# The last layer of a graph network: Strassen's seven products in place of eight, per pair of row tiles

## The reference

```python
h = relu(layernorm(x));  x = x + L0(h, adj)     # (A @ (h W0 + b0)) / column sums
h = relu(layernorm(x));  x = x + L1(h, adj)     # normalised A + I, relu
h = relu(layernorm(x));  x = x + L2(h, adj)     # attention over adj
h = relu(layernorm(x));  x = x + L3(h, adj)
# L3: head = mask / sqrt(row sum of mask); inc = adj + head
#     return (inc @ h) / sum(inc)               # = adj @ h times one factor per row
```

## Time and profile before

| | |
|---|---|
| median of 3 runs | 1386.33 us (1385.8 to 1390.24) |
| profiled execution, own time | 1388.27 us |
| its span | 1386.4 us |
| busy: PE, weight loads, DVE, ACT, POOL | 1344.6, 1023.1, 861.2, 528.8, 118.5 us |

### The profile page before, as it was taken

How to read it: one execution, slowest core, us unless ns; L and a number is a source line. 1 busy time by engine, 2 the same in 40 slices (tenths; PEclk the granted TensorE clock), 3 DMA queues, 4 the chain that set the end, 5 groups by cost and what they waited for, 6 DMA issues and landing times.

```text
span 1386.4 us, 26434 instructions
## 1 busy us (share of the span) xinstructions
PE 1344.6 (97%) x10252; PEld 1023.1 (74%) x10252; DVE 861.2 (62%) x1776; ACT 528.8 (38%) x1240; POOL 118.5 (9%) x193
## 2 busy tenths in 40 slices
PE   4899999989999999999999999999999999999999
PEld 3688888864555555567777777777777777888887
DVE  5799888958355555577677767767777886000000
ACT  3487544726222222344444544544545553000000
POOL 1100000012323222210000000000000000000000
PEclk8899999999999999999999999999999999999999
DMA  9999999720121120101110111110111003232221
GB/s 225 254 314 348 378 378 379 288 81 16 61 61 52 56 62 1 62 24 32 31 31 24 31 39 32 31 31 24 32 39 32 16 24 122 85 92 85 84 85 31
DMA packets 52812, 141.19 MB, mean 102 GB/s; under 512 B 7632, under 2 KB 16848, under 8 KB 52688
## 3 DMA queue, kind: packets, MB, share of 16 engines
q1 hardware_dynamic: 50288, 137.39, 31.2%
q10 hardware_dynamic: 2400, 2.10, 0.4%
HBM read 118.49 MB, written 20.97 MB: 101 GB/s over the span
## 4 chain that ended last, share of the span: by engine, by line
PE 88%; DVE 6%; DMA 2%; SPq 1%; issue 1%; ACT 1%; POOL 0%; DVEq 0%; ACTq 0%
PE ps L1336 16%; PE ps L1337 16%; PE ps L1350 11%; PE ps L1237 8%; PE ps L1238 8%; PE ps L1199 7%; PE ps L1200 7%; PE ps L1367 4%; PE ps L1386 4%; PE ps L1398 4%; DMA acc<-in_adj 2%; DVE ring L625 1%; SPq L307 1%; PE ps L1216 1%; PE ps L1295 1%
## 5 line engine op out<-in xcount | busy, mean ns | idle before, releaser
L1199 PE MATMUL ps<-val_hi,ring 128*128 128x257 f16 x1024 | 226.6, 274 | 0.0
L1200 PE MATMUL ps<-val_lo,ring 128*128 128x256 f16 x1024 | 226.5, 273 | 0.0
L1337 PE MATMUL ps<-acc,ring 128*128 128x256 f16 x1024 | 225.8, 273 | 0.0
L1336 PE MATMUL ps<-acc,ring 128*128 128x256 f16 x1024 | 225.8, 271 | 0.0
L1237 PE MATMUL ps<-ring,acc 128*128 128x512 fp8e4 x512 | 194.9, 381 | 4.0 <-DVE acc L762 3.9
L1350 PE MATMUL ps<-hnt 128*128 128x512 f16 (+3 forms) x864 | 196.3, 363 | 0.0
L1238 PE MATMUL ps<-ring,acc 128*128 128x512 fp8e4 x512 | 194.8, 380 | 0.0
L625 DVE STREAM_TRANSPOSE ring<-acc 128x1024 uint8<-128x1024 uint8 x128 | 151.5, 1219 | 27.1 <-DMA acc<-in_adj 26.9
L1142 ACT ACTIVATE ring<-ring 128x512 f16<-128x512 f32 (+2 forms) x133 | 79.3, 596 | 227.1 <-DVE ring L897 226.8
L897 DVE SCALAR_TENSOR_TENSOR ring<-ring,ps 128x512 f32<-128x512 fp8e4 (+2 forms) x133 | 85.7, 645 | 117.5 <-PE ps L1386 117.5
L1336 PE MATMUL ps<-val_hi,hs 128*128 128x257 f16 x534 | 145.8, 273 | 0.6 <-DVE hs L878 0.6
(11 more groups left out here) (166 smaller groups left out, 2104.4 us busy)
## 6 DMA issues: line engine op xcount, KB each, us to landing
acc<-in_adj SPq DMA_DIRECT2D x256, 256.0 KB, 7.7
ring<-at_dram SPq DMA_DIRECT2D x56, 512.0 KB, 3.9
at_dram<-ring SPq DMA_DIRECT2D x32, 512.0 KB, 8.9
ring<-at_dram SPq DMA_DIRECT2D x64, 256.0 KB, 2.9
xs<-in_x SPq DMA_DIRECT2D x12, 256.0 KB, 11.9
out<-xs ACTq DMA_DIRECT2D x14, 128.0 KB, 3.9
out<-xs SPq DMA_DIRECT2D x14, 128.0 KB, 3.1
xs<-in_x SPq DMA_DIRECT2D x8, 128.0 KB, 2.9
```

What stands on the lines that cost most here:

```text
L1199: nc.tensor.matmul(ps[:, k % 8, 0:D + 1], lhs, val_hi0[:, t, 0:D + 1], start=(t == 0), stop=False)
L1200: last = nc.tensor.matmul(ps[:, k % 8, 0:D], lhs, val_lo0[:, t, :], start=False, stop=(t == NB - 1))
L1336: nc.tensor.matmul(ps[:, bank, 0:n], lhs, hi[:, t, 0:n], start=start, stop=False)
L1337: return nc.tensor.matmul(ps[:, bank, 0:D], lhs, lo[:, t, :], start=False, stop=stop)
```

## The change

Row tiles are taken in 16 pairs `n`, one tile of group 2p and the one at the same place in group 2p + 1. The blocks of even and of odd value tiles make with the two row tiles a 2 x 2 matrix, the even and odd value tiles with their left and right 128 columns another. Strassen's scheme multiplies these with seven products instead of eight. A product is 16 matmuls of 256 moving columns (128 high, 128 low).

- Four of the seven stationary operands are differences of adjacency blocks (`d5`, `d1`, `d2`, and `a21`, `a12` changed in place): the 8-bit numbers are so coded that masks and exclusive or on 32-bit words give the differences. For pairs of groups p = 0 part of this stands in attention steps (`PREP`), the rest after the tails; for p > 0 it stands between the products.
- The moving operands are the values and five sums of them, made in f32 with the rows (`make_sums`) and split in high and low (`sums_high`, `sums_low`). The tail has 17 items instead of 15.
- The results are put together by ACT (four copies out of PSUM), GpSimd (two differences) and DVE.
- The adjacency is loaded in 16 pieces of 1 MB, each in runs of 512 bytes.
- Semaphores of the statistics are merged, which changes no order.

```diff
-        TAIL = 15
+        TAIL = 17
-            per = 1 if length > TAIL else 2 if length > GB else 3
+            per = 1 if length >= TAIL else 2 if 2 * length >= TAIL else 3
+        PREP = {}
+        for r in range(4):
+            PREP[16 + 4 * r] = ("mask", "a11", r)
+            PREP[17 + 4 * r] = ("sign", "a11", r)
+            PREP[18 + 4 * r] = ("mask", "a22", r)
+            PREP[19 + 4 * r] = ("sign", "a22", r)
+            PREP[NB + 17 + r] = ("d5", "d5", r)
+            PREP[NB + 21 + r] = ("d7", "a12", r)
...
+            sp.wait_ge(sem["pv1_done"], NS)
+            for k in ("11", "22", "12"):
+                load_raw(sp, 1, k)
...
+                if n % GB == GB - 1 and n // GB + 2 < NG // 2:
+                    sp.wait_ge(sem["products_done"], 4 * n + 4)
+                    load_raw(sp, n // GB + 2, "11")
+                    load_raw(sp, n // GB + 2, "22")
...
+            def make_sums(k):
+                nc.vector.tensor_tensor(sums32[k % 2][:, P:3 * P], even, odd, ALU.add)
+                nc.vector.scalar_tensor_tensor(sums32[k % 2][:, 3 * P:5 * P].rearrange("p (s d) -> p s d", s=2), both[:, :, 0:P], -1.0,
+                                               both[:, :, P:D], ALU.mult, ALU.subtract)
+                nc.vector.tensor_tensor(sums32[k % 2][:, 0:P], even[:, 0:P], odd[:, P:D], ALU.subtract).then_inc(sem["sums_made"], 1)
...
+            def dif2(p):
+                if p > 0:
+                    dve.wait_ge(sem["three_done"], GB * p)
...
+            def first_differences(n):
+                dve.wait_ge(sem["products_done"], 4 * n + 2)
+                dve.wait_ge(sem["copied"], 4 * n + 4)
...
+            dif2(0)
+            dif1(0)
+            dif6(0)
...
+            for n in range(NB // 2):
+                p, i = n // GB, n % GB
+                last = p == NG // 2 - 1
+                if p > 0 and i == 0:
+                    dif7(p)
+                    if not last:
+                        edge_mask(p + 1, "a11")
+                elif i == 1 and p > 0 and not last:
+                    edge_mask(p + 1, "a22")
+                    sign(p + 1, "a11")
+                    sign(p + 1, "a22")
+                elif i == 2 and p > 0 and not last:
+                    dif5(p + 1)
+                    dif1(p + 1)
+                elif i == 3 and not last:
+                    if p == 0:
+                        dif5(1)
+                        dif1(1)
+                    dif2(p + 1)
+                    if p > 0:
+                        dif6(p + 1)
+                first_differences(n)
+                if n == 0:
+                    edge_mask(1, "a11")
+                elif n == 1:
+                    edge_mask(1, "a22")
...
+                two_tiles(n)
...
+            def last_four(n):
...
+                since(pe, sem["tiles_step"], 8 * (n - 1) + 7)
+                pe.wait_ge(sem["difs_done"], 3 * p + 2)
...
+                pe.wait_ge(sem["tiles_step"], 8 * n + 2)
+                pe.wait_ge(sem["dif7_done"], made(p))
...
+                for k in range(12):
+                    pe.wait_ge(sem["lo3_done"], k + 1)
+                    for m in range(3):
+                        multiply(n, m, k)
+            for k in range(12, NB // 2):
+                pe.wait_ge(sem["lo3_done"], k + 1)
+                for n in range(3):
+                    for m in range(3):
```

More of the change, by code:

```diff
@@ L123, in gnn_kernel @@
         h1 = [hs[:, i * D:(i + 1) * D] for i in range(4)]
+        sums32 = [w_all[:, i * 5 * P:(i + 1) * 5 * P] for i in range(2)]
+        rows_a = hs[:, 0:2 * D].rearrange("p (h d) -> p h d", h=2)
+        rows_b = hs[:, 2 * D:4 * D].rearrange("p (h d) -> p h d", h=2)
+        copies = [w_all[:, j * D:(j + 1) * D].rearrange("p (h d) -> p h d", h=2) for j in range(4)]
         late = ring[:, 7 * N:7 * N + 2048].bitcast(F32)
@@ L553, in _ @@
                 nc.gpsimd.tensor_tensor(rstd4[g % 2], ve4[g % 2], half[:, 0:GB], ALU.pow).then_inc(sem["rstd3_ready"], 1)
+            for n in range(NB // 2):
+                pool.wait_ge(sem["copied"], 4 * n + 2)
+                since(pool, sem["tiles_step"], 8 * n)
+                nc.gpsimd.tensor_tensor(rows_a[:, :, P:D], copies[1], copies[0], ALU.subtract).then_inc(sem["side_done"], 1)
+                pool.wait_ge(sem["copied"], 4 * n + 4)
+                nc.gpsimd.tensor_tensor(rows_b[:, :, 0:P], copies[3], copies[2], ALU.subtract).then_inc(sem["side_done"], 1)
         @block.vector
@@ new lines, in dif7, with prepare @@
+            def dif7(p, r=None):
+                dve.wait_ge(sem["dif5_done"], made(p) if r is None else r + 1)
+                dve.wait_ge(sem["negated"], negated(p, "a22"))
+                nc.vector.tensor_tensor(words(kept[p]["a12"], r), words(kept[p]["a12"], r), words(kept[p]["a22"], r),
+                                        ALU.bitwise_xor).then_inc(sem["dif7_done"], 1)
+            def prepare(n):
+                what, k, r = PREP[n]
+                if what == "mask":
+                    edge_mask(0, k, r)
+                elif what == "sign":
+                    sign(0, k, r)
+                elif what == "d5":
+                    dif5(0, r)
+                else:
+                    dif7(0, r)
@@ L979, in _ @@
                     add_mirror(n - 1)
+                if n in PREP:
+                    prepare(n)
                 if n in late_at["transposes_n"]:
@@ new lines, in _ @@
+            for i in range(5, 7):
+                group_tail(NG - 1, i)
+            group_tail(NG - 2, 13)
+            for i in range(7, 10):
+                group_tail(NG - 1, i)
+            group_tail(NG - 2, 14)
+            group_tail(NG - 1, 10)
+            group_tail(NG - 2, 15)
+            group_tail(NG - 2, 16)
+            for i in range(11, TAIL):
+                group_tail(NG - 1, i)
+            dve.wait_ge(sem["t_done"], n_mirrored[NS])
+            dif2(0)
+            dif1(0)
@@ new lines, in _ @@
+            dif6(0)
+            dve.wait_ge(sem["f3_ready"], 1)
+            for n in range(NB // 2):
+                p, i = n // GB, n % GB
[23 more added lines that the diff above has]
+                    edge_mask(1, "a22")
+                elif n == 2:
+                    sign(1, "a11")
+                    sign(1, "a22")
+                elif n == 3:
+                    dif6(1)
+                two_tiles(n)
@@ new lines, in multiply, with first_three @@
+            def multiply(n, m, k):
+                name, rows, j = FACTORS[m]
+                i = n % GB
+                lhs = homes[kept[n // GB][name]][:, k // 8, k % 8, i * P:(i + 1) * P]
+                return nc.tensor.matmul(product(n, j), lhs, moving(rows, k), start=(m in (0, 2, 4, 5, 6) and k == 0),
+                                        stop=(m in (1, 3, 4, 5, 6) and k == NB // 2 - 1))
+            def first_three(n):
+                p = n // GB
+                since(pe, sem["copied"], 4 * (n - 3) + 4)
+                pe.wait_ge(sem["negated"], negated(p, "a22"))
+                pe.wait_ge(sem["dif5_done"], made(p))
```

359 lines of the change are left out of this document (242 added, 117 removed).

## The result

| | before | after |
|---|---|---|
| median of the runs, us | 1386.48 (1385.80 to 1390.24, 4 runs) | 1378.39 (1375.27 to 1379.09, 4 runs) |
| span of the profiled execution, us | 1386.4 | 1377.3 |
| ratio after / before | | 0.9926, 95% interval 0.991 to 0.9942 |

A forecast was written before the change was run, and what follows sets the result against it. It took PE's 2048 matmuls to bound the last layer and DVE the stretch before it. The terms -28.2 + 4.2 + 6.5 + 1.7 + 3.3 + 0.9 made -11.6 us, giving 1374.7 us, range 1364.5 to 1383.5.

The forecast's parts named there:

- Matmuls: Last layer: 1792 matmuls in place of 2048, 256 fewer at 0.1103 us each, -28.2 us.
- Price of 2048 words: DVE operations of 2048 words: 2.2 us from start to start, 4.4 as the bound from above.
- Mid-attention: Middle of attention: added DVE work (`PREP`, tail items of groups 1 to 5) hides in waits for PE, 0 us.
- Group 6's steps: Attention, group 6: tail items packed three to a step, with round trips to GpSimd and ACT, delay DVE, +4.2 us.
- Handover: Start of the last layer: PE waits for three low halves, then `dif2`, `dif1` and `dif6`, +6.5 us.
- clock: Handover stretch: PE's gaps lower the granted clock for 5 us, +1.7 us, bounds 0 and 4.
- Pairs 1 to 3: Last layer, early tile pairs: DVE's differences and tiles and ACT's stores make PE wait, +3.3 us, bounds 0 and 6.
- Pairs 4 to 15: Rest of the last layer: PE needs 12.35 us a pair, DVE 9.1, loads of 1 MB land in 5.9; 0 us.
- more is hidden: Rival: group 6 costs 2, handover 5, clock and pairs 1 to 3 nothing; -20.3 us, 1366 us; chance 0.17.
- the clock stays low: Rival: clock low through handover and pairs 0 to 2, matmuls there take double; 1386 us, no change; chance 0.08.
- loads of short runs are slow: Rival: adjacency loads in the last layer take 11.6 us each, +8 us, 1383 us; chance 0.1.
- DVE becomes the bound: Rival: 2048-word operations take 4.4 us, so DVE needs 14.05 us a pair against 12.35; 1403 us; chance 0.06.

The follow-up runs named there:

- e_hand: The changed kernel with the handover's tail items in another order and the rows of k = 14 in a buffer of their own; median 1374.6 us.
- e_nosums: The changed kernel without the four sums of quadrants and their low halves in DVE's tails (output not the reference's); median 1371.3 us.
- e_stores: The changed kernel with ACT issuing a tile pair's output stores behind the next pair's copies; median 1373.4 us.
- e_slack: The changed kernel with one unneeded DVE reduction over 2048 elements in each tile pair from the fifth on; median 1387.1 us.
- e_tail: The changed kernel with tail items packed by a table and ACT making a group's second pair of rows right behind the first sums' high parts; median 1376.8 us.
- e_order: The changed kernel with `dif2` and `dif6` of the next four pairs put behind the first differences; median 1374.9 us.

## Why the prediction was right, step by step

- **Matmuls, -28.2.** Right: 1792 of them, weight loads never in the way.
- **Price of 2048 words, 2.2 us.** Right alone (2.28 to 2.29 in the traces). Unforeseen was 2.7 to 2.81 beside GpSimd. `sign`, which has one input, took 1.22 us, as the Trainium skill has it (VectorE: DVE Perf Modes, "The perf-mode tier table", 1227 ns); I had kept 2.2, and this hid an error. From the two `sign` to the first differences of pair 3, for which PE waited 1.05 us, DVE never stood idle:

```profile
1210.23 2.35 DVE L1091 TENSOR_SCALAR val_hi<-val_hi 128x2048 int32<-128x2048 int32 x2
...
1217.37 2.29 DVE L1107 SCALAR_TENSOR_TENSOR ring<-val_hi 128x2048 int32<-128x2048 int32 x1
1219.57 2.81 DVE L1116 TENSOR_TENSOR ring<-val_lo,val_hi 128x2048 int32<-128x2048 int32 x1
1222.31 0.41 DVE L1151 TENSOR_TENSOR hs<-ps,w_all 128x256 f32<-128x256 f32 x1
```

  At 2.2 us each, this wait would have been about 2 us longer (an estimate from these rows).
- **Mid-attention, 0.** Right for `PREP` and the tails of groups 1 to 3: the ends of groups 1, 2 and 3 stand where they did, to 0.02 us. Wrong at its end: the sentence "the tail items of groups 1 to 5 cost at most 0.88 in a step of one item" overlooked that 17 items no longer fit one by one into group 4's 16 steps. There they go two by two, as they did in group 5 before the change already, and groups 4 and 5 rose by 0.6 each.
- **Group 6's steps, +4.2.** Measured +5.3, less 0.3 in group 7. The mechanism was right, the two round trips of 1.12 and 1.16 us stand where they were put; the size was off by 0.8, and DVE waited once for PE there (0.73 us at 1149.05), where no such wait was foreseen.
- **Handover, +6.5, and clock, +1.7.** The low halves came as said: 0.50, 1.89 and 1.69 us against 0.55, 1.95 and 1.9. The waits for the three differences (2.1) did not come, because the clock lost 3.4 us and not 1.7 and covered them. The two terms make 7.5 us in place of 8.2. In e_hand and e_nosums, where the clock stays up, the three waits are there.
- **Pairs 1 to 3, +3.3.** Measured 3.0, but by two errors that cancel. ACT's stores were put at 0.5 us, and with the stores out of the way 2.5 of the 3.0 us went (e_stores); the two `sign` were put at 4.4 us in DVE's queue and took 2.35. That the sum came out is luck.
- **Pairs 4 to 15, 0.** 1.07 us at pairs 7 and 11, the pairs that were named as the worst with a lead of 0.2 us; GpSimd's 0.4 us in `dif6` used that up. The load that `edge_mask` of p = 2 waits for and the one that `edge_mask` of p = 3 waits for landed in 6.3 us each (estimated 5.9); DVE waited 0.59 and 2.67 for them, PE not at all.
- **The end, +0.9.** Right.

The last layer was forecast at 209 us and lasted 209.0, partly by errors that cancel: 0.7 too much in the handover, 0.3 in pairs 1 to 3 (itself the rest of two errors of about 2 us), 1.1 too little in pairs 7 and 11. The time came 3.7 us above the forecast: 1.9 from the start of the last layer (groups 4 to 7 together +6.1 against +4.2), 0.7 from ahead of attention, and the rest is how the runs' median lies to the profiled execution (0.7 below it here, 1.9 in the kernel before).

Of the rivals, "more is hidden" failed in group 6 and in the handover; "the clock stays low" came true for some 7 us (0.81 and 0.51 in two stretches of 5), not through to pair 2; "loads of short runs are slow" is refuted by the two that landed in 6.3 us and not 11.6; "DVE becomes the bound" is refuted by 2.29 us per operation and by e_slack, in which eight pairs of twelve took another 2.3 us. What remains open: why the same waits cost 3.4 us of clock in the changed kernel and e_tail and 1.7 in e_order and e_stores, and why the clock is low at the start of attention in seven executions of fourteen, with equal code ahead of it.

## What to carry to other kernels

- When work is added to a list that is dealt out over steps, recompute the packing for every length, not only for the one that looks tight: a rule such as one item per step flips to two at 16 against 17.
- A helper engine's items are free only at the point of its order where it idles. Find that point in its own waits before moving them; a few places further the same items cost about 12 us.
- Gaps of PE of about 2 us close together are the first to remove: two cost 3.6 us as waits and up to 3.4 more as clock, and one reordering took the second part away while the sum of the waits stayed.
